# Attention on one Trainium2 core: the product of the probabilities with the values of a key block as one piece of up to 512 columns

## The chip, the core and the metric

The kernel runs on one NeuronCore of a Trainium2 chip. The core has TensorE (PE in the rows, with its weight loads as PEld), VectorE (DVE), ScalarE (ACT), GpSimdE (POOL) and SyncE (SP), which issues most DMAs. The metric is the device time of one execution in microseconds (us); lower is better. The times given are medians of several executions.

## The reference

The program is a small transformer stack on x of shape (1, 2048, 256): attention "a" (rotary, 16 query heads on 4 key heads), a feed-forward block with 4-bit weights, attention "b" (16 heads on 16), and the same feed-forward block again, each behind a layer norm and added to x. The change is in the attention, which both layers share:

```python
scores = jnp.einsum('bthd,bshd->bhts', q, k) * scale
causal = jnp.tril(jnp.ones((S, S), dtype=bool))
scores = jnp.where(causal[None, None, :, :], scores, -jnp.inf)
probs = jax.nn.softmax(scores, axis=-1)
attended = jnp.einsum('bhts,bshd->bthd', probs, v).reshape(B, S, hidden)
```

S is 2048, a head has 16 numbers, and all arithmetic is float32.

## The kernel before

**Tiles.** The 16 heads are worked in 4 groups g of 4 heads, the 2048 queries in 4 tiles t of 512. Groups follow each other with the tiles in the order 0, 1, 2, 3, then 3, 2, 1, 0, and so on. Keys are cut into blocks kb of 128; tile t needs blocks 0 to 4t+3, since attention is causal. In the last four of them queries below the block see none of its keys, so the block has only 512, 384, 256 or 128 columns there.

**Two passes over the scores.** The softmax needs each query's maximum before the exponential. So the scores are computed twice.

- M (line 856): queries by keys, for the maximum. One M is one head, 128 queries against a chunk of up to 512 keys. Two heads together make a pair: both halves of one slot of `ring`, and one VectorE reduction of 128x1024 (line 1071) reads them. `ring` has two slots, taken in turn, so the first half of a pair waits until the pair two before it has been reduced (`slot`, `pe.wait_ge(s_rd, n - 1)`). Chunks on the diagonal are 128 to 512 wide and get two small mask matmuls (line 860).
- S (line 882): keys by queries, 128 keys of one head against up to 512 queries, with the maximum folded in. ScalarE turns it into `probs` (line 976). S takes one of three banks `ps_s`; it waits for the exponential of the S three before it.
- PV (line 899): values times probabilities, one matmul per head, 4 heads side by side on 32 output rows each, added up over the key blocks in `ps_o`. A PV matmul is in float32, which the program turns into two records, so a piece of four heads shows as x8 in the trace.
- O (line 908): four transposes of the finished tile, through a slot of `ring`; VectorE divides (lines 1083 and 1086).

**The order of the work.** `attention_plan` writes one list of all this; each engine walks through it in order and issues its own part. A step is one key block: four S, one per head. While tile t is in its S pass, the M of the next tile are laid between its S, and the function `ahead` sets how many. From tile 3 of group 0 to the end of group 2, which is 96 steps in each layer, there is one M behind every S: the first half of a pair stands behind the S of heads 1 and 3, the second half behind the S of heads 2 and 0. In group 3 there are fewer and in its last two tiles none.

PV for a key block stands two steps behind its S. It is cut in two pieces of 256 columns: piece 0 ahead of the S of head 0, piece 1 ahead of the S of head 2. In the last two blocks of a tile only piece 1 is there, of 256 and of 128 columns; the block before them has a piece 0 of 128 columns.

Of the kernel before, what the change touches and what calls it, by code (L numbers as in the profile page):

```python
# [30 lines left out]
TW = 512  # L31
NT = S // TW
BT = TW // P
# [290 lines left out]
def attention_plan(extra):  # L324

    order = [(g, t) for g in range(NG) for t in (range(NT) if g % 2 == 0 else range(NT - 1, -1, -1))]
    pairs = [("M", g, t, qb, p, c) for g, t in order for qb in range(BT) for p in range(2) for c in range(t + 1)]
    first, ends, total = [], [], 0
    for g, t in order:
        first.append(total)  # L330
        total += BT * GH * (t + 1)
        ends.append(total)

    def ahead(s):
        tail = len(order) - NT
        if s < first[1]:
            return min(ends[1], LEAD + (ends[1] - LEAD) * s // (first[1] - 6))
        for k in range(1, len(order) - 1):
            if first[k] <= s < first[k + 1] and (k < NT - 1 or k >= tail):
                start, end = ends[k] + (SLACK if k > 1 else 0), ends[k + 1] + SLACK  # L340
                return min(total, start + (end - start) * (s - first[k]) // (first[k + 1] - first[k]))
        return min(total, max(e + SLACK - max(f - s, 0) for e, f in zip(ends, first)))

    plan, made, rows, turns = [], 0, [], []

    def after(x):
        if x[3:6] == (BT - 1, 1, x[2]):
            rows.append([("R", x[1], x[2]), 2 if x[1:3] == (0, 0) else 4])

    def pass_rows():  # L350
        for r in list(rows):
            r[1] -= 1
            if r[1] < 0:
                plan.append(r[0])
                rows.remove(r)

    def both_halves():
        x = pairs[made // 2]
        plan.extend([x + (0,), x + (1,)])
        after(x)  # L360
        pass_rows()
        return made + 2

    def pass_turns():
        for o in turns:
            o[1] -= 1

    def opening(t, counts, beside=(), after_turn=()):
        nonlocal made
        laid = relayout(t - 1, extra) if t else []  # L370
        items = projection(t, extra)
        for k, y in enumerate(items):
            plan.extend(laid[k] if k < len(laid) else [])
            plan.append(y)
            if k == 0:
                plan.extend(beside)
            if k == len(items) - 3:
                plan.extend([("TU", t + 1), *after_turn])
            for _ in range(counts[k - len(items)] if counts else 0):
                made = both_halves()  # L380

    plan += [("LS", 0), ("LC", 0, 1), ("N", 0), ("LS", 1)] + ([("W", 0)] if extra else [("F", 40)])
    plan += [("TU", 0), ("F", 12), ("LC", 1, 2), ("N", 1)]
    opening(0, [], [("LS", 2)], [("LS", 3), ("LC", 2, 4), ("N", 2)])
    opening(1, [0, 0, 2, 2], [], [("N", 3)])
    opening(2, [2, 2, 2, 2] if extra else [2, 3, 3])
    later = {}
    laid, items = relayout(NT - 2, extra), projection(NT - 1, extra)
    for k, y in enumerate(items):
        later[k * BT * GH // len(items)] = (laid[k] if k < len(laid) else []) + [y]  # L390
    for k, x in enumerate(relayout(NT - 1, extra)):
        later[BT * GH + 2 + 4 * k] = x
    turned = {30: ("WL", 1), 36: ("W", 1), 42: ("WL", 2), 50: ("W", 2), 56: ("WL", 3), 64: ("W", 3)} if extra else {}
    late, due, s, step = [], [], 0, 0
    for g, t in order:
        for kb in range(BT * (t + 1)):
            chunk, place = divmod(step - 13, 9)
            if extra and 0 <= chunk < NF and place == 0:
                plan.append(("X", chunk))
            k = step % (BT * NT * (NT + 1) // 2) - (3 if g else 8)  # L400
            if g + 1 < NG and 0 <= k < LOADS:
                plan.append(("LD", g + 1, k))
            if step in turned:
                due.append(turned[step])
            done = late.pop(0) if len(late) == LATE else None
            for h in range(GH):
                if done and h % 2 == 0:
                    at = done[2] - BT * done[1]
                    if at < 2 or h == (0 if at == BT - 1 else 2):
                        plan.append(("PV",) + done + (1 if at >= 2 else h // 2,))  # L410
                    if h:
                        pass_turns()
                    if h == 0 and at == BT - 1:
                        turns.append([("O",) + done[:2], 3])
                while rows and rows[0][0][1:] == (g, t):
                    pass_rows()
                due += later.get(s, [])
                if made % 2 == 0:
                    plan += due + [o for o, n in turns if n < 0]
                    due, turns = [], [o for o in turns if o[1] >= 0]  # L420
                plan.append(("S", g, t, kb, h))
                if made < ahead(s) or made % 2:
                    x = pairs[made // 2]
                    plan.append(x + (1 - h % 2,))
                    made += 1
                    if made % 2 == 0:
                        after(x)
                s += 1
                pass_rows()
                while made % 2 == 0 and made + 1 < ahead(s) - 1:  # L430
                    if g == 0:
                        plan.append(("FM", 2))
                    made = both_halves()
            if extra and chunk >= 0 and place == 8:
                plan.extend([("T", chunk, 0), ("T", chunk, 1)])
            late.append((g, t, kb))
            step += 1
    for done in late:
        for half in range(2):
            if half or done[2] - BT * done[1] < 2:  # L440
                plan.append(("PV",) + done + (half,))
    return order, plan + [o for o, _ in turns] + [("O",) + order[-1]]


# [82 lines left out]
def attention_block(nc, io, per, layer):  # L527
    rope = layer == "a"
    extra = rope
    with ExitStack() as ctx:  # L530
# [59 lines left out]
        order, plan = attention_plan(extra)  # L590
# [21 lines left out]
        half = [slice(HALF * h, HALF * (h + 1)) for h in range(2)]  # L612
# [32 lines left out]
        def width(t, kb):  # L645

            return P * max(0, kb - BT * t)
# [108 lines left out]
        def _(pe):  # L756
# [25 lines left out]
            for y in plan:  # L782
# [17 lines left out]
                elif y[0] == "TU":  # L800
                    t = y[1]
# [6 lines left out]
                elif y[0] == "PJ":  # L808
                    _, t, f = y
# [3 lines left out]
                    for a in range(2):  # L813
                        at, count = feats(f) if rope else ((2 * f + a) * P, P)
# [6 lines left out]
                elif y[0] == "VJ":  # L821
                    t = y[1]
                    out = slot(y)
                    at = 2 * P + 64 if rope else 4 * P
# [5 lines left out]
                elif y[0] == "RL":  # L830
                    _, t, f, a = y
                    n = part_no(("PJ", t, f))
                    b = n % NST
                    if n == 0:
# [7 lines left out]
                              start=False, stop=True).then_inc(s_s, 1)  # L842
                elif y[0] == "M":
                    _, g, t, qb, p, c, h = y
# [13 lines left out]
                    if c == t:  # L858
                        for a in range(2):
                            op = pe.matmul(out[:, h, w - P:w], ident[half[h], a, :], above[half[h], a, :],  # L860
                                           start=False, stop=a == 1)
                    if y in ends:
                        op.then_inc(s_rf, 1)
                elif y[0] == "R":
                    _, g, t = y
# [7 lines left out]
                elif y[0] == "S":  # L873
                    _, g, t, kb, h = y
                    out = bank(y)
                    if kb == 0 and h == 0:
# [7 lines left out]
                                   start=True, stop=not diagonal)  # L884
                    if diagonal:
                        for a in range(2):
                            op = pe.matmul(out[:, 0:P], ident[half[h % 2], a, :], below[half[h % 2], a, :],  # L887
                                           start=False, stop=a == 1)
                    op.then_inc(s_s, 1)
                elif y[0] == "PV":  # L890
                    _, g, t, kb, part = y
                    pe.wait_ge(s_e, scored[("S", g, t, kb, GH - 1)] + 1)
                    if kb == 0:
                        pe.wait_ge(s_ot, rank[g, t])
                    c = slice(max(width(t, kb), TW // 2 * part), TW // 2 * (part + 1))
                    n = pvs[y[:4]]
                    for h in range(GH):
                        v = vg[g][:, kb, 0:VC] if shared else vg[g][:, kb, h * VC:(h + 1) * VC]
                        last = pe.matmul(ps_o[32 * h:32 * h + VC, c], v, pr[n % NPR][:, h, c],  # L899
                                         start=kb == 0 and part == 0, stop=kb == BT * (t + 1) - 1)  # L900
                    if part:
                        last.then_inc(s_pv, 1)
                elif y[0] == "O":
                    _, g, t = y
                    pe.wait_ge(s_ot, rank[g, t] + 1)
                    out = slot(y)
                    for b in range(BT):
                        last = pe.transpose(out[:, 0, b * P:(b + 1) * P], ot[:, b * P:(b + 1) * P], per["ident"][:, :])
                    last.then_inc(s_rf, 1)
# [567 lines left out]
```

## Time and profile before

| | |
|---|---|
| median of 3 executions | 1894.46 us (1891.48 to 1908.91) |
| time of the profiled execution | 1903.19 us |
| its span, first to last instruction | 1901.3 us |
| mean granted TensorE clock | 0.946 |
| busy: PE, PEld | 1761.2 us (93%), 1135.2 us (60%) |
| busy: DVE, ACT, POOL | 1156.9 us (61%), 957.5 us (50%), 545.9 us (29%) |
| PE matmul records | 13822 |
| PV (line 899), records | 4608 |

"Span" is the time between the first and the last instruction of the profiled execution; the execution's own time is 1.9 us more. Busy is the time in which at least one instruction of the engine is under way. Matmuls are pipelined, so a busy PE is not a PE at its peak: the time that an instruction costs is better read from the distance between starts.

### The profile page before, as it was taken

How to read it: one execution, taken by the hardware profiler on the slowest of the kernel's cores; microseconds unless marked ns; L12 is line 12 of the kernel's file. 1: busy time of each engine (PE TensorE's matmuls, PEld its weight loads, DVE VectorE, ACT ScalarE, POOL GpSimd, SP SyncE). 2: the span in 40 equal slices, each digit the busy share in tenths (PEclk: the TensorE clock that was granted, in tenths of full speed). 3: DMA queues.
4: the chain of work that ended last, by engine and by line, in shares of the span. 5: the costliest groups of instructions: out<-in, count | busy, mean ns of one | idle time of the engine just before them, and what ended most of it. 6: DMA issues, size and time to landing. Idle time of an engine off the chain costs nothing. (4 is left out here: it accounts for less than half of the span.)

```text
span 1901.3 us, 34086 instructions
## 1 busy us (share of the span) xinstructions
PE 1761.2 (93%) x13822; PEld 1135.2 (60%) x13822; DVE 1156.9 (61%) x1702; ACT 957.5 (50%) x1901; POOL 545.9 (29%) x466
## 2 busy tenths in 40 slices
PE   7799999999999879999987999999999997999998
PEld 5554444554445568888865644445544446888887
DVE  5446777677875266444465477776777626654444
ACT  2133566666777524434332245776667872444333
POOL 5211566576677602223220010000000000223222
PEclk8786889999999889999998889999999998999999
DMA  5103305125011060000003223060330004100000
GB/s 130 50 27 42 54 22 104 40 55 87 23 42 39 34 266 1 1 1 0 0 1 117 84 37 54 10 82 2 44 48 2 2 2 201 66 12 1 11 11 11
DMA packets 49391, 86.04 MB, mean 45 GB/s; under 512 B 20856, under 2 KB 34936, under 8 KB 46984
## 3 DMA queue, kind: packets, MB, share of 16 engines
q1 hardware_dynamic: 44472, 67.84, 15.5%
q0 software_dynamic: 4256, 15.78, 2.7%
q8 instruction: 97, 1.59, 0.4%
q10 hardware_dynamic: 528, 0.52, 0.1%
q14 instruction: 38, 0.31, 0.1%
HBM read 55.02 MB, written 28.84 MB: 44 GB/s over the span
## 5 line engine op out<-in xcount | busy, mean ns | idle before, releaser
L1071 DVE TENSOR_REDUCE chunk_max<-ring 128x2 f32<-128x1024 f32 (+3 forms) x640 | 674.0, 1064 | 276.0 <-PE ring L856 162.8
L976 ACT ACTIVATE probs<-ps_s 128x512 f32<-128x512 f32 (+3 forms) x1280 | 624.1, 534 | 343.2 <-PE ps_s L887 177.5
L1404 POOL TENSOR_TENSOR inter_lo<-inter,inter_hi 128x512 fp32r<-128x512 f32 x128 | 165.4, 1292 | 935.4 <-ACT inter_hi L1338 935.4
L856 PE MATMUL ring<-unit_rounded 63*128 63x512 f32 (+3 forms) x640 | 246.1, 479 | 26.6 <-DVE chunk_max L1071 8.9
L856 PE MATMUL ring<-region_rounded 63*128 63x512 f32 (+3 forms) x640 | 254.9, 447 | 5.1 <-DVE chunk_max L1071 4.5
L882 PE MATMUL ps_s<-unit_rounded 64*128 64x512 f32 (+3 forms) x640 | 252.7, 446 | 5.4 <-ACT probs L976 4.2
L882 PE MATMUL ps_s<-region_rounded 64*128 64x512 f32 (+3 forms) x640 | 228.9, 441 | 4.3 <-ACT probs L976 4.2
L1378 DVE SCALAR_TENSOR_TENSOR gelu_a<-gelu_a,ps_g 128x512 f32<-128x512 f32 x128 | 87.9, 687 | 183.9 <-ACT gelu_a L1332 183.6
L882 PEld LDWEIGHTS ps_s<-unit_rounded 64*128 64x128 f32 x640 | 112.5, 195 | 138.8 <-ACT probs L976 105.9
L1332 ACT ACTIVATE gelu_a<-ps_g 128x512 f32<-128x512 f32 x128 | 76.5, 598 | 229.4 <-PE ps_u L94 229.2
L899 PE MATMUL ps_o<-probs,unit_plain 128*32 128x256 f32 (+1 forms) x2304 | 186.9, 398 | 0.0
L899 PE MATMUL ps_o<-probs,region_plain 128*32 128x256 f32 (+1 forms) x2304 | 177.3, 380 | 0.0
L882 PEld LDWEIGHTS ps_s<-region_rounded 64*128 64x128 f32 x640 | 101.8, 184 | 126.5 <-ACT probs L976 102.9
L92 PE MATMUL ps_d<-w_mlp,inter_lo 128*128 128x256 f32 x512 | 150.2, 293 | 28.8 <-DVE x L1369 15.2
L94 PE MATMUL ps_d<-w_mlp,inter_hi 128*128 128x256 f32 x512 | 145.3, 284 | 0.0
L93 PE MATMUL ps_d<-w_mlp,inter_hi 128*128 128x256 f32 x512 | 144.9, 283 | 0.0
L856 PEld LDWEIGHTS ring<-unit_rounded 63*128 63x128 f32 x640 | 104.8, 195 | 64.0 <-DVE chunk_max L1071 21.9
L1345 ACT ACTIVATE gelu_b<-gelu_a 128x512 f32<-128x512 f32 x128 | 80.9, 632 | 118.5 <-DVE gelu_a L1378 118.5
L1383 DVE SCALAR_TENSOR_TENSOR gelu_b<-gelu_b,ps_g 128x512 f32<-128x512 f32 x128 | 87.9, 687 | 85.3 <-ACT gelu_b L1345 85.3
L860 PE MATMUL ring<-mask_above,half_ident 64*128 64x128 bf16 x1024 | 138.3, 228 | 0.0
L887 PE MATMUL ps_s<-mask_below,half_ident 64*128 64x128 bf16 x1024 | 133.3, 225 | 0.0
L92 PEld LDWEIGHTS ps_d<-w_mlp,inter_lo 128*128 128x128 f32 x512 | 97.6, 191 | 52.7 <-POOL inter_lo L1404 31.4
(184 smaller groups left out, 2980.3 us busy)
## 6 DMA issues: line engine op xcount, KB each, us to landing
w_mlp<-w_scr SPq DMA_DIRECT2D x32, 768.0 KB, 14.6
w_scr<-region_rounded POOLq DMA_DIRECT2D x16, 768.0 KB, 3.9
region_rounded<-q_scr SPq DMA_DIRECT2D x24, 256.0 KB, 8.3
q_scr<-region_rounded SPq DMA_DIRECT2D x16, 192.0 KB, 2.3
unit_rounded<-q_scr SPq DMA_DIRECT2D x12, 256.0 KB, 8.9
q_scr<-region_rounded SPq DMA_DIRECT2D x8, 384.0 KB, 3.6
k_scr<-region_rounded SPq DMA_DIRECT2D x8, 384.0 KB, 3.6
v_scr_b<-region_plain SPq DMA_DIRECT2D x4, 768.0 KB, 3.7
```

What stands on the lines that cost most here:

```text
L92: pe.matmul(out, ll, rh, start=start, stop=False)
L93: pe.matmul(out, lh, rl, start=False, stop=False)
L94: return pe.matmul(out, lh, rh, start=False, stop=stop)
L856: op = pe.matmul(out[:, h, 0:w], qt[g][plain[h], p, q0:q0 + P], kt[g][plain[h], p % NKP, c * TW:c * TW + w], start=True, stop=c < t)
L860: op = pe.matmul(out[:, h, w - P:w], ident[half[h], a, :], above[half[h], a, :], start=False, stop=a == 1)
L882: op = pe.matmul(out[:, 0:TW - w0], kt[g][shifted[h % 2], (h // 2) % NKP, kb * P:(kb + 1) * P], qt[g][shifted[h % 2], h // 2, t * TW + w0: ...
L887: op = pe.matmul(out[:, 0:P], ident[half[h % 2], a, :], below[half[h % 2], a, :], start=False, stop=a == 1)
L899: last = pe.matmul(ps_o[32 * h:32 * h + VC, c], v, pr[n % NPR][:, h, c], start=kb == 0 and part == 0, stop=kb == BT * (t + 1) - 1)
L976: act.activation(pr[n % NPR][:, h, w0:TW], src[:, 0:TW - w0], ACT.Exp, scale=SCALE).then_inc(s_e, 1)
L1071: dve.tensor_reduce(mp[rank[y[1:3]] % 2][:, qb, 2 * p:2 * p + 2, c], ring[n % 2][:, :, 0:w], AX.X, ALU.max).then_inc(s_rd, 1)
L1378: dve.scalar_tensor_tensor(out=ta[b][:, :], in0=ta[b][:, :], scalar=1.0, in1=ps_g[b][:, :], op0=ALU.add, op1=ALU.mult).then_inc(s_arg, 1)
L1404: pool.tensor_tensor(il[n % NI][:, :], ti[n % 2][:, :], ih[n % NI][:, :].bitcast(F32), ALU.subtract).then_inc(s_il, 1)
```

## The change

The two pieces of a key block's PV become one, ahead of the S of head 0, with 512 columns, or 384, 256 or 128 in the last four blocks of a tile. So the PV of the third block on the diagonal, which was one piece ahead of the S of head 2, moves ahead of the S of head 0 as well. Everything else stands in the list where it stood. Each layer has 160 pieces where it had 288.

```diff
             for h in range(GH):
-                if done and h % 2 == 0:
+                if done and h == 0:
                     at = done[2] - BT * done[1]
-                    if at < 2 or h == (0 if at == BT - 1 else 2):
-                        plan.append(("PV",) + done + (1 if at >= 2 else h // 2,))
-                    if h:
-                        pass_turns()
-                    if h == 0 and at == BT - 1:
+                    plan.append(("PV",) + done + (1,))
+                    if at == BT - 1:
                         turns.append([("O",) + done[:2], 3])
+                if done and h == 2:
+                    pass_turns()
...
     for done in late:
-        for half in range(2):
-            if half or done[2] - BT * done[1] < 2:
-                plan.append(("PV",) + done + (half,))
+        plan.append(("PV",) + done + (1,))
...
-                    c = slice(max(width(t, kb), TW // 2 * part), TW // 2 * (part + 1))
+                    c = slice(width(t, kb), TW)
                     n = pvs[y[:4]]
                     for h in range(GH):
...
-                                         start=kb == 0 and part == 0, stop=kb == BT * (t + 1) - 1)
+                                         start=kb == 0, stop=kb == BT * (t + 1) - 1)
```

TensorE's instructions in the stage with one M per S, layer b, group 2, tile 2, from the S of head 1 of one step to that of head 0 two steps on. `ps_s0` to `ps_s2` are the three banks of S, `ring0` and `ring1` the two slots of the pairs, `ps_o` is PV. Before:

```order
L882 MATMUL ps_s2_8<-unit_rounded_8 128x512
L856 MATMUL ring1_8<-unit_rounded_8 128x512
L899 MATMUL ps_o_8<-probs_8,unit_plain_8 32x256 x4
L882 MATMUL ps_s0_8<-unit_rounded_8 128x512
L856 MATMUL ring1_8<-unit_rounded_8 128x512
L882 MATMUL ps_s1_8<-unit_rounded_8 128x512
L856 MATMUL ring0_8<-unit_rounded_8 128x512
L899 MATMUL ps_o_8<-probs_8,unit_plain_8 32x256 x4
L882 MATMUL ps_s2_8<-unit_rounded_8 128x512
L856 MATMUL ring0_8<-unit_rounded_8 128x512
```

The change at the same place:

```order
L879 MATMUL ps_s2_8<-unit_rounded_8 128x512
L853 MATMUL ring1_8<-unit_rounded_8 128x512
L879 MATMUL ps_s0_8<-unit_rounded_8 128x512
L853 MATMUL ring1_8<-unit_rounded_8 128x512
L879 MATMUL ps_s1_8<-unit_rounded_8 128x512
L853 MATMUL ring0_8<-unit_rounded_8 128x512
L896 MATMUL ps_o_8<-probs_8,unit_plain_8 32x512 x4
L879 MATMUL ps_s2_8<-unit_rounded_8 128x512
L853 MATMUL ring0_8<-unit_rounded_8 128x512
```

Before, each of the two slots has a piece of PV between the first and the second half of its pair. In the change the pair in `ring1` has none between its halves, and the pair in `ring0` has the whole piece of 512 columns.

The second place is on TensorE too: layer b, group 3, tile 1, where no M are left. Before:

```order
L899 MATMUL ps_o_8<-probs_8,region_plain_8 32x256 x4
L882 MATMUL ps_s2_8<-region_rounded_8 128x512
L882 MATMUL ps_s0_8<-region_rounded_8 128x512
L899 MATMUL ps_o_8<-probs_8,region_plain_8 32x256 x4
L882 MATMUL ps_s1_8<-region_rounded_8 128x512
L882 MATMUL ps_s2_8<-region_rounded_8 128x512
L899 MATMUL ps_o_8<-probs_8,region_plain_8 32x256 x4
```

The change at the same place:

```order
L896 MATMUL ps_o_8<-probs_8,region_plain_8 32x512 x4
L879 MATMUL ps_s2_8<-region_rounded_8 128x512
L879 MATMUL ps_s0_8<-region_rounded_8 128x512
L879 MATMUL ps_s1_8<-region_rounded_8 128x512
L879 MATMUL ps_s2_8<-region_rounded_8 128x512
L896 MATMUL ps_o_8<-probs_8,region_plain_8 32x512 x4
```

All four S of a step now follow one another, and the fourth is written to the bank of the first (`ps_s2`).

## Rows read from the trace of the kernel before

**Rows 1.** The page: its head and the busy time of each engine.

```profile
span 1901.3 us, 34086 instructions
PE 1761.2 (93%) x13822; PEld 1135.2 (60%) x13822; DVE 1156.9 (61%) x1702; ACT 957.5 (50%) x1901; POOL 545.9 (29%) x466
```

**Rows 2.** Windows: stretch, length, busy time of each engine, granted clock.

```profile
core 0: us, PE busy (x) PEld busy (x) DVE busy (x) ACT busy (x) POOL busy (x), PEclk, DMA share, GB/s
...
237.70:541.00 303.30, 294.45 (x2900) 152.16 (x2897) 229.19 (x264) 206.54 (x425) 202.59 (x146) 0.97 0.26 55
...
1059.40:1182.60 123.20, 113.62 (x902) 57.79 (x901) 82.64 (x83) 53.85 (x108) 7.57 (x3) 0.90 0.31 54
1182.60:1466.50 283.90, 276.23 (x2821) 141.05 (x2817) 213.38 (x221) 195.68 (x403) 0.00 (x0) 1.00 0.23 31
1466.50:1539.30 72.80, 71.84 (x775) 34.96 (x773) 42.84 (x47) 57.67 (x117) 0.00 (x0) 1.00 0.01 2
```

**Rows 3.** Waits: who waited for whom; us in total, times, longest.

```profile
PEld ring L856 <- DVE chunk_max L1071: 40.2, 98, 2.0
...
PE ring L856 <- DVE chunk_max L1071: 13.4, 38, 1.7
```

**Rows 4.** Timeline of PE, layer b: start, us, engine, line, operation, names, shapes.

```profile
1403.03 0.50 PE L882 MATMUL ps_s<-unit_rounded 64*128 64x512 f32 x1
1403.03 0.73 PE L856 MATMUL ring<-unit_rounded 63*128 63x512 f32 x2
1403.37 0.40 PE L882 MATMUL ps_s<-unit_rounded 64*128 64x512 f32 x1
...
1404.84 0.48 PE L882 MATMUL ps_s<-unit_rounded 64*128 64x512 f32 x1
1404.88 0.49 PE L856 MATMUL ring<-unit_rounded 63*128 63x512 f32 x1
1405.30 0.64 PE L899 MATMUL ps_o<-probs,unit_plain 128*32 128x256 f32 x8
...
1405.87 0.49 PE L856 MATMUL ring<-unit_rounded 63*128 63x512 f32 x1
```

**Rows 5.** Timeline of DVE in the same stretch.

```profile
1403.60 1.23 DVE L1071 TENSOR_REDUCE chunk_max<-ring 128x2 f32<-128x1024 f32 x1 [0.39 <-PE ring L856]
```

**Rows 6.** Timeline of DVE, layer b, group 2, tile 3; x2 are two in a row.

```profile
1423.64 2.36 DVE L1071 TENSOR_REDUCE chunk_max<-ring 128x2 f32<-128x1024 f32 x2 [0.59 <-PE ring L856]
1426.48 1.95 DVE L1071 TENSOR_REDUCE chunk_max<-ring 128x2 f32<-128x1024 f32 x2 [0.48 <-PE ring L856]
1429.32 2.46 DVE L1071 TENSOR_REDUCE chunk_max<-ring 128x2 f32<-128x1024 f32 x2 [0.89 <-PE ring L856]
1432.17 1.96 DVE L1071 TENSOR_REDUCE chunk_max<-ring 128x2 f32<-128x1024 f32 x2 [0.40 <-PE ring L856]
...
1435.75 2.46 DVE L1071 TENSOR_REDUCE chunk_max<-ring 128x2 f32<-128x1024 f32 x2 [0.83 <-PE ring L856]
```

**Rows 7.** Timeline of PE: a piece of 128 columns and what follows it.

```profile
1382.12 0.43 PE L899 MATMUL ps_o<-probs,unit_plain 128*32 128x128 f32 x8
1382.47 0.32 PE L882 MATMUL ps_s<-unit_rounded 64*128 64x128 f32 x1
```

**Rows 8.** Timeline of PE in group 3, tile 1, where no M are left.

```profile
1548.56 0.64 PE L899 MATMUL ps_o<-probs,region_plain 128*32 128x256 f32 x8
1549.13 0.51 PE L882 MATMUL ps_s<-region_rounded 64*128 64x512 f32 x2
...
1549.70 0.64 PE L899 MATMUL ps_o<-probs,region_plain 128*32 128x256 f32 x8
```

**Rows 9.** Timeline of ACT in the stretch of rows 4.

```profile
1403.56 0.60 ACT L976 ACTIVATE probs<-ps_s 128x512 f32<-128x512 f32 x1 [0.53 <-PE ps_s L882]
```

**Rows 10.** Timeline of PE at a granted clock of 0.5 (1.2 GHz).

```profile
1107.68 1.08 PE L899 MATMUL ps_o<-probs,unit_plain 128*32 128x256 f32 x8
1108.69 0.79 PE L882 MATMUL ps_s<-unit_rounded 64*128 64x512 f32 x1
```

## The prediction, made before the changed kernel was run

> **What bounds the kernel now.** The page comes first [rows 1]: PE is busy 93% of the span and every other engine 61% or less. The list of waits seems to confirm that: PE's matmuls wait for VectorE's reduction in only 38 places, 13.4 us, and its weight loads 40.2 us [rows 3]. Read so, a change that takes work off PE gains. The windows show which stage counts [rows 2]: group 0 from its tile 3 to the end of group 2 takes 303.3 us in layer a and 283.9 us in layer b for 96 steps each, so 3.16 and 2.96 us a step, at clock 0.97 and 1.00. VectorE is busy 213 of the 283.9 us there, so it isn't the bound by its sum.
>
> The timeline says what is. Follow one slot of `ring` [rows 4, 5]. The second half of a pair starts at 1403.03; VectorE begins its reduction at 1403.60 and ends it at 1404.83; the first half of the next pair in that slot starts at 1404.88; PV starts at 1405.30, and the second half at 1405.87. That closes a loop: 0.57 + 1.23 + 0.05 + 0.42 + 0.57 = 2.84 us, and it allows one step per turn, since each slot serves one pair a step. PE shows as busy all this time, since its records overlap (the M of 1404.88 lasts 0.49 us, PV starts 0.42 behind it) and S runs beside a late M; so the wait hardly shows as idle PE. The reductions of tile 3 in group 2 begin at 1423.64, 1426.48, 1429.32, 1432.17 [rows 6]: 2.84, 2.84, 2.85 us, the loop to the hundredth, with VectorE idle for 0.4 to 0.9 us ahead of each. So the stage is bound by a latency round PE and VectorE, and PV's duration is a term of it.
>
> **What the change does to PE's own work.** A piece of 256 columns takes 1405.30 to 1405.87, 0.569 us before rounding; one of 128 takes 1382.12 to 1382.47, 0.356 us [rows 4, 7]. So 128 columns cost 0.213 us and a piece 0.143 us besides. One of 512 columns is then 0.569 + 2 x 0.213 = 0.995 us; 384 gives 0.782. No row shows a piece of 512. Its bounds are 0.569 + 0.213 = 0.78 us, if only half of the added columns cost, and 2 x 0.569 = 1.14, if nothing is saved; I take 0.995, since two widths fix the line. 256 pieces go (2 x 128), so PE alone would save 256 x 0.143 = 36.6 us.
>
> The Trainium skill (TensorEngine Tiling, "Key Properties") says that a change of tiling mode drains TensorE. By that page each piece between S and S pays such a drain, and the whole change would be worth its 256 drains. The trace agrees that there is a fixed part, 0.143 us a piece.
>
> **What it does to the loop.** The order shows it: the pair of one slot has no PV between its halves any more, the pair of the other has all 512 columns. Its loop is 0.57 + 1.23 + 0.05 + 0.42 + 0.995 = 3.27 us. The light slot's is 0.57 + 1.23 + 0.05 + 0.34 (S to S, 1403.03 to 1403.37) = 2.19 us, but a step ends only when both are done. PE does nothing in between: the waiting M stands ahead of PV in PE's queue, and behind PV all S. So a step goes from 2.84 to 3.27 us, +0.43, where the heavy slot's pair is a full one.
>
> I counted by the order over the 192 steps of this stage (two layers), with the step lengths from the starts of S in the trace:
> - 108 steps with a full pair in the heavy slot and 512 columns, without O. 74 last 2.83 to 2.98 us now; they become 3.27: 74 x 0.41 = +30. The other 34 last 3.09 to 5.9 us, because masks, layer a's unpacking on VectorE or a tile's change add to them; they get +0.43 at the most and -0.143 at the least. I take 0, since 3.27 is about what they take already.
> - 14 steps with O, which takes a slot of its own, so the first half waits for the pair just before: 1432.17 to 1435.75 is 3.58 us [rows 6]. The longer PV lies behind that wait too: 14 x 0.43 = +6.
> - 16 steps with a full pair and a PV of 256 columns, which moves from the S of head 2 to that of head 0, into the heavy loop: from 2.35 to 2.84 us, +0.49 each, +8.
> - 12 with a full pair and 384 columns (0.57 + 1.23 + 0.05 + 0.42 + 0.78 = 3.05, now 2.80): +3.
> - 42 others, with short pairs or a PV of 128 columns; 22 of them have 512 or 384 columns and save 0.143: -3.
>
> Stage: +44 us.
>
> **The rest.** Group 0's tiles 0 to 2 take 123.2 us in layer b for 24 steps [rows 2], with up to four pairs a step. If PE bounds them, 18 steps a layer save 0.143 us (-5 in all); if a slot's loop with PV in it does, 24 of the 48 lose up to 0.43 (+10). I take +3, between the two. In group 3 the three banks of S take over. Half a step without M lasts 1.14 us [rows 8], a step 2.28. After: the exponential starts 0.53 us behind its S (1403.03 to 1403.56) and lasts 0.60 [rows 9]; the fourth S needs its bank, so it starts at 0.53 + 0.60 + 0.05 = 1.18 us; PV follows 0.34 later, taken as from S to S, then 0.995: 2.51 us. That is +0.23 in 12 steps, +3. Where M are left, 28 steps a layer take 72.8 us in layer b [rows 2], 2.60 each; the 44 with 512 columns come to 2.51, -4. ScalarE pays nothing else: PV's own inputs are exponentials of two steps back. Both feed-forward phases and the projections don't change.
>
> Sum: 44 + 3 + 3 - 4 = +46 us on the profiled execution's 1903.2 us. That one is 8.7 us above the median, which is 1894.5; taken on the median it gives **1941 us**.
>
> **Rivals.**
> - *The gain arrives* (0.08). If the loop had slack, for instance because M could be issued under a running PV, the time is 1894.5 - 36.6 = 1858 us. For it: PE's 93%. Against it: starts 2.84 us apart with VectorE idle. It decides from the point where a 512-column loop fits under a step's own work on PE, which is 4 x 0.34 + 0.995 = 2.4 us. The Trainium skill (Perfetto Trace Analysis, "Matmuls") holds larger matmuls to be more efficient where they are possible; it speaks for this rival, and rows 6 speak against it.
> - *Gain and loss cancel* (0.12). The 74 steps pay, but PE-bound steps save the whole 0.143 wherever they can: 30 - (256 - 74) x 0.143 = +4, so 1899 us, and up to 1913.
> - *The clock falls too* (0.06). PE's idle share grows in each step. At 1.2 GHz a piece of 256 takes 1107.68 to 1108.69, 1.01 us, not 0.57 [rows 10]; one of 512 about 1.86. The loop is then 0.87 longer, and with slower S and M 1.1. A third of the 192 steps at it is 70 us more: about 2012 us. Against it: the stage runs at clock 1.00 now, though some of its steps take 4 us and more.
> - *The forecast* (0.74): the long PV sits in one slot's loop. Its own range: with only the 74 steps paying and a saving in all other 82 merged pieces of the stage, 30 - 12 = +18, so 1912; with all 122 full steps at +0.43 (52), +11 for the moved and shortened pieces, +10 early and +3 late, +76, so 1971.
>
> **How the numbers follow.** The range 1908 to 1972 holds the forecast's range and the upper part of the cancelling case; it leaves out the gain, the clock and the rest of that case, 0.2. About 1%, 19 us, is what a measurement of this kernel can tell from no change. Slower by more: the forecast and the clock, 0.80; within: the cancelling case, 0.12; faster: 0.08.
>
> **What would show it.** In the new profile: PV in 2560 records, a piece of 512 columns 0.995 us from its start to the next S; reductions of 1024 columns in group 2, tile 3 that come in twos, 3.27 us apart, with more than 0.8 us idle ahead; that tile, now 46.3 us, at 51 or more; PE waiting more for line 1071 than the 53.6 us of rows 3; in group 3, tile 1, steps near 2.5 us and ScalarE no longer the engine without gaps. I am wrong if steps there come in under 2.84 us, or if PV of 512 columns costs under 0.6 us.

## The result and the profile after

| | before | the change |
|---|---|---|
| median | 1892.97 us (1891.39 to 1908.91, 4 executions) | 1951.14 us (1948.78 to 1955.25, 4 executions) |
| ratio to before | | 1.0278, 95% interval 1.0226 to 1.0330 |
| profiled execution, its span | 1903.19 us, 1901.3 us | 1948.78 us, 1946.9 us |
| mean granted clock | 0.946 | 0.955 |

The kernel is 2.8% slower. Line numbers are lower by 3: M is line 853, S 879, PV 896, the exponential 973, the pairs' reduction 1068. The page of the change, its head, its busy row, and the groups of the reduction and of the two sorts of M. A group shows busy time and mean ns, and then the idle time ahead of it with its releasers:

```profile
span 1946.9 us, 29958 instructions
...
PE 1741.7 (89%) x11774; PEld 1100.6 (57%) x11774; DVE 1135.6 (58%) x1702; ACT 937.0 (48%) x1901; POOL 545.8 (28%) x466
...
L1068 DVE TENSOR_REDUCE chunk_max<-ring 128x2 f32<-128x1024 f32 (+3 forms) x640 | 656.8, 1061 | 335.8 <-PE ring L853 237.3
...
L853 PE MATMUL ring<-unit_rounded 63*128 63x512 f32 (+3 forms) x640 | 219.9, 455 | 39.8 <-DVE chunk_max L1068 20.4
L853 PE MATMUL ring<-region_rounded 63*128 63x512 f32 (+3 forms) x640 | 237.1, 428 | 20.3 <-DVE chunk_max L1068 17.6
```

PE has 2048 matmul records less than in [rows 1] and is busy 19.5 us less; it did save work. Yet the span grew by 45.6 us, and every engine's share fell. The list of waits says who waits for whom:

```profile
PEld ps_s L879 <- ACT probs L973: 270.5, 442, 1.7
DVE chunk_max L1068 <- PE ring L853: 237.3, 229, 7.4
...
PEld ring L853 <- DVE chunk_max L1068: 86.9, 175, 0.8
...
PE ring L853 <- DVE chunk_max L1068: 38.0, 143, 0.6
```

PE now waits 86.9 + 38.0 = 124.9 us for the reductions, where [rows 3] had 53.6, and VectorE waits 237.3 us for M, where it was 162.8. Each waits for the other: a loop.

Windows of the change, with the columns of rows 2: layer a from group 0, tile 3 to the end of group 2; layer b's group 0, tiles 0 to 2; the same stage in layer b; and the two tiles of group 3 with M.

```profile
226.00:552.10 326.10, 292.10 (x2278) 143.04 (x2274) 219.83 (x264) 200.35 (x425) 205.55 (x147) 0.99 0.24 52
1070.80:1194.20 123.40, 109.47 (x764) 53.83 (x763) 82.38 (x83) 53.29 (x109) 7.58 (x3) 0.92 0.32 54
1194.20:1504.60 310.40, 277.89 (x2198) 133.36 (x2194) 205.91 (x221) 188.97 (x402) 0.00 (x0) 1.00 0.21 28
1453.40:1504.60 51.20, 45.84 (x338) 20.40 (x334) 34.78 (x36) 32.04 (x66) 0.00 (x0) 1.00 0.00 1
1504.60:1578.40 73.80, 70.37 (x582) 32.08 (x578) 42.26 (x46) 55.32 (x116) 0.00 (x0) 1.00 0.01 1
```

Against [rows 2] the stage takes 326.1 instead of 303.3 us in layer a and 310.4 instead of 283.9 in layer b: +22.8 and +26.5, together more than the 45.6 us by which the span grew. Layer b's early tiles are as long as they were (123.4 and 123.2 us). The fourth row is group 2, tile 3 alone, 51.2 us. VectorE, in that tile:

```profile
1456.60 2.36 DVE L1068 TENSOR_REDUCE chunk_max<-ring 128x2 f32<-128x1024 f32 x2 [1.07 <-PE ring L853]
1459.87 1.82 DVE L1068 TENSOR_REDUCE chunk_max<-ring 128x2 f32<-128x1024 f32 x2 [0.92 <-PE ring L853]
1463.14 2.36 DVE L1068 TENSOR_REDUCE chunk_max<-ring 128x2 f32<-128x1024 f32 x2 [1.44 <-PE ring L853]
1466.40 1.82 DVE L1068 TENSOR_REDUCE chunk_max<-ring 128x2 f32<-128x1024 f32 x2 [0.91 <-PE ring L853]
```

The twos start 3.27, 3.27 and 3.26 us apart, with 0.91 to 1.44 us idle ahead; they were 2.84 apart [rows 6]. One such step on PE:

```profile
1461.15 0.49 PE L853 MATMUL ring<-region_rounded 63*128 63x512 f32 x1 [0.17 <-DVE chunk_max L1068]
1461.57 1.07 PE L896 MATMUL ps_o<-probs,unit_plain 128*32 128x512 f32 x8
1462.57 0.49 PE L879 MATMUL ps_s<-unit_rounded 64*128 64x512 f32 x1
1462.57 0.73 PE L853 MATMUL ring<-region_rounded 63*128 63x512 f32 x2
1462.91 0.62 PE L879 MATMUL ps_s<-unit_rounded 64*128 64x512 f32 x2
...
1463.75 0.50 PE L879 MATMUL ps_s<-unit_rounded 64*128 64x512 f32 x1 [0.21 <-ACT probs L973]
1464.42 0.49 PE L853 MATMUL ring<-region_rounded 63*128 63x512 f32 x1 [0.17 <-DVE chunk_max L1068]
```

The waiting first half comes at 1461.15 and again at 1464.42, 3.27 us later. PV takes 1461.57 to the second half at 1462.57, 1.00 us. The reduction starts at 1463.14, 0.57 us behind it, and the next first half follows its end. There is a second wait in the same step: the fourth S (1463.75) waits for the exponential that frees its bank. Counted over the program, the S that start within 75 ns of that end were 66 before and are 239 now. This wait comes first and is covered by the reduction's: the same wait stands in e1 below, where a step takes 2.61 us and not 3.27.

To compare the stages I added up all steps by the starts of S, both layers, in each profile ("early" is group 0, tiles 0 to 2; "main" the stage of 192 steps with an M behind every S; "group 3" runs to the start of its last step). The experiments are in the same table:

| kernel | early | main | group 3 | median us |
|---|---|---|---|---|
| before | 260.3 | 587.2 | 201.8 | 1892.97 |
| the change | 247.4 | 636.4 | 210.1 | 1951.14 |
| e1, one piece ahead of S of head 1 | 235.6 | 534.4 | 208.9 | 1833.7 |
| e2, two pieces ahead of S of heads 1, 3 | 220.7 | 526.6 | 205.7 | 1803.26 |
| e3, two pieces ahead of S of head 0 | 259.6 | 647.0 | 209.4 | 1951.35 |
| e5, a longer reduction | 314.7 | 732.0 | 209.6 | 2106.39 |
| e6, one piece in group 3 only | 258.8 | 587.0 | 210.7 | 1906.6 |
| e8, one piece ahead of S of head 2 | 249.0 | 611.8 | 209.1 | 1922.89 |
| e9, e2 with the block of 384 as one piece | 222.3 | 528.5 | 203.9 | 1808.15 |

### The profile page after: what moved, and what is told of

Its sections match the earlier page's. It is cut to its first block and busy times, and to the rows that moved or that the text cites. A ratio compares the mean times of both kernels' runs of the same rounds, so it can differ in the third digit from the quotient of the medians.

```text
span 1946.9 us, 29958 instructions
## 1 busy us (share of the span) xinstructions
PE 1741.7 (89%) x11774; PEld 1100.6 (57%) x11774; DVE 1135.6 (58%) x1702; ACT 937.0 (48%) x1901; POOL 545.8 (28%) x466
## 5 line engine op out<-in xcount | busy, mean ns | idle before, releaser
L1068 DVE TENSOR_REDUCE chunk_max<-ring 128x2 f32<-128x1024 f32 (+3 forms) x640 | 656.8, 1061 | 335.8 <-PE ring L853 237.3
L973 ACT ACTIVATE probs<-ps_s 128x512 f32<-128x512 f32 (+3 forms) x1280 | 602.2, 538 | 402.2 <-PE ps_s L879 214.2
L853 PE MATMUL ring<-unit_rounded 63*128 63x512 f32 (+3 forms) x640 | 219.9, 455 | 39.8 <-DVE chunk_max L1068 20.4
L853 PE MATMUL ring<-region_rounded 63*128 63x512 f32 (+3 forms) x640 | 237.1, 428 | 20.3 <-DVE chunk_max L1068 17.6
L879 PE MATMUL ps_s<-unit_rounded 64*128 64x512 f32 (+3 forms) x640 | 234.9, 424 | 12.6 <-ACT probs L973 10.1
L896 PE MATMUL ps_o<-probs,unit_plain 128*32 128x512 f32 (+3 forms) x1280 | 155.5, 559 | 0.0
L896 PE MATMUL ps_o<-probs,region_plain 128*32 128x512 f32 (+3 forms) x1280 | 152.6, 551 | 0.0
L853 PEld LDWEIGHTS ring<-unit_rounded 63*128 63x128 f32 x640 | 99.6, 189 | 85.0 <-DVE chunk_max L1068 44.9
L853 PEld LDWEIGHTS ring<-region_rounded 63*128 63x128 f32 x640 | 109.0, 185 | 50.6 <-DVE chunk_max L1068 42.0
L857 PE MATMUL ring<-mask_above,half_ident 64*128 64x128 bf16 x1024 | 131.2, 226 | 0.0
```

Of the source, the lines that this page charges most:

```text
L853: op = pe.matmul(out[:, h, 0:w], qt[g][plain[h], p, q0:q0 + P], kt[g][plain[h], p % NKP, c * TW:c * TW + w], start=True, stop=c < t)
L879: op = pe.matmul(out[:, 0:TW - w0], kt[g][shifted[h % 2], (h // 2) % NKP, kb * P:(kb + 1) * P], qt[g][shifted[h % 2], h // 2, t * TW + w0: ...
L973: act.activation(pr[n % NPR][:, h, w0:TW], src[:, 0:TW - w0], ACT.Exp, scale=SCALE).then_inc(s_e, 1)
L1068: dve.tensor_reduce(mp[rank[y[1:3]] % 2][:, qb, 2 * p:2 * p + 2, c], ring[n % 2][:, :, 0:w], AX.X, ALU.max).then_inc(s_rd, 1)
```

## The experiments

The theory: PV's duration is a term of the loop second half, reduction, first half, PV, second half in one slot. What counts is where the long piece stands, not that it is one piece. The rivals: joining costs something by itself (the drain, PE's queue), or the loss is in another wait (the banks of S).

**e1: the one piece elsewhere.** Behind S of head 0 comes a second half, behind S of head 1 a first one. So a piece ahead of the S of head 1 lies between two pairs, and between the halves of none.

```diff
-                if done and h == 0:
+                if done and h == 1:
```

> The change with the one piece moved by one place: it stands ahead of the S of head 1, where no pair of M is open, and all else stays. Theory (PV's length is a term of the loop of the slot whose pair it stands in): no pair has PV between its halves, so from a second half to the next first half of that slot there are 2.0 us of other work, more than the 1.84 us of the wait. A full step is then set by PE, the three banks of S or VectorE's two reductions, about 2.5 us, not 3.27: the stage with one M per S falls from 636 us to about 530, the time from 1951 to about 1845 us. Rival (the longer matmuls or the run of four S cost by themselves, wherever they stand): 1951 us, within 10.

Measured: 1833.7 us (1828.1 to 1839.1), ratio 0.9676 [0.9594, 0.9759] to before, whose median beside it was 1901.6. The piece is the same as in the change, and four S still follow one another; the place is the only difference. It is worth 117 us by the medians, 114 by the ratios (before's median was 1893.0 us beside the change). One step in e1, group 2, tile 3, on PE (lines as in the change):

```profile
1359.62 0.50 PE L879 MATMUL ps_s<-unit_rounded 64*128 64x512 f32 x1
...
1360.81 0.50 PE L879 MATMUL ps_s<-unit_rounded 64*128 64x512 f32 x1 [0.22 <-ACT probs L973]
...
1361.25 1.06 PE L896 MATMUL ps_o<-probs,unit_plain 128*32 128x512 f32 x8
1362.24 0.50 PE L879 MATMUL ps_s<-unit_rounded 64*128 64x512 f32 x1
```

No M waits in this step; what is left is the bank. The S of 1360.81 waits for its bank, 1.19 us behind the first of the four; PV follows 0.44 later and lasts 0.99: 2.62 us. The median of the full steps is 2.61.

**e2: the two pieces elsewhere.** The kernel before, with its pieces ahead of the S of heads 1 and 3, so each lies between two pairs, and S is spread evenly too.

```diff
-                if done and h % 2 == 0:
+                if done:
                     at = done[2] - BT * done[1]
-                    if at < 2 or h == (0 if at == BT - 1 else 2):
+                    if h % 2 and (at < 2 or h == (1 if at == BT - 1 else 3)):
                         plan.append(("PV",) + done + (1 if at >= 2 else h // 2,))
-                    if h:
+                    if h == 2:
                         pass_turns()
```

> The kernel before with its two pieces moved by one place each, ahead of the S of heads 1 and 3, so that no pair has PV between its halves; nothing is joined. Theory: the loop of 2.84 us is gone, a full step takes about 2.5 us (PE's own 2.47), the time falls from 1893 to about 1845 us. Rival (before was bound by PE's own work, not by the loop): 1893 us, within 5.

Measured: 1803.26 us (1802.2 to 1807.9), ratio 0.9515 [0.9438, 0.9592]. It is the fastest of all, 4.9% below before. The expectation was 1845 us and missed by 42: it counted the full steps of the main stage, but the table gives 60.6 us there and 39.6 in the early tiles. Part of those 39.6 is the clock. Not all is: in e6, whose code is that of before in these tiles, layer b's early tiles take 115.0 us at a clock of 1.00, and in e2 105.6 at 0.97. So PV's place counts there too. On PE, group 2, tile 3 (lines as before):

```profile
1339.99 0.50 PE L882 MATMUL ps_s<-unit_rounded 64*128 64x512 f32 x1
1339.99 0.73 PE L856 MATMUL ring<-region_rounded 63*128 63x512 f32 x2
1340.33 0.40 PE L882 MATMUL ps_s<-unit_rounded 64*128 64x512 f32 x1
1340.66 0.64 PE L899 MATMUL ps_o<-probs,unit_plain 128*32 128x256 f32 x8
1341.23 0.50 PE L882 MATMUL ps_s<-unit_rounded 64*128 64x512 f32 x1
```

Half a step is 1.24 us, a step 2.48, and no row has a wait: 4 x 0.335 for the S with their M and 2 x 0.569 for PV are 2.48. In such a step PE's own work is the bound. Such steps are only a part of the stage: the 108 steps that are full ones in the change have a median of 2.60 us in e2, 2.61 in e1, since the masks of a diagonal chunk and waits add to others; what bounds those was not taken apart. PE's window over that tile, with the columns of rows 2:

```profile
1322.50:1364.10 41.60, 41.53 (x449) 19.35 (x445) 36.26 (x36) 33.09 (x66) 0.00 (x0) 1.00 0.01 2
```

PE is busy 41.53 of 41.60 us, but it was busy 45.15 of 46.30 in the same tile of before, so this alone would not tell. Over the whole span its share is 93%, just what it is in [rows 1] at a span 101 us longer.

**e3: two pieces, both where the change has its one.** This takes joining and place apart.

```diff
-                if done and h % 2 == 0:
+                if done and h == 0:
...
-                    if at < 2 or h == (0 if at == BT - 1 else 2):
-                        plan.append(("PV",) + done + (1 if at >= 2 else h // 2,))
+                    plan.extend([("PV",) + done + (half,) for half in range(0 if at < 2 else 1, 2)])
```

> The move without the joining: both pieces of 256 columns stand ahead of the S of head 0, one behind the other. Theory: the loop holds 2 x 0.569 us of PV if a piece pays its fixed 0.143 us behind another piece too: full steps 3.41 us, 0.14 more than the change, the time about 1975 us. If the fixed part is paid only at a change between S and PV (a drain at the mode's change), full steps 3.27 us and 1951 us. Rival (the joining is what costs, not the place): near 1893 us.

Measured: 1951.35 us (1946.8 to 1966.1), ratio 1.0280 [1.0196, 1.0363]. That is the time of the change. (In the table e3's main stage is 10.6 us longer than the change's; in its profile the clock was 0.85 in group 2, tile 3, where the change had 1.00, and that tile took 56.4 us, not 51.2; other tiles of its layer b stage had a lower clock too.) Both pieces on PE in e3:

```profile
1456.13 1.07 PE L899 MATMUL ps_o<-probs,unit_plain 128*32 128x256 f32 x16
1457.13 0.44 PE L882 MATMUL ps_s<-unit_rounded 64*128 64x384 f32 x1
```

Two pieces back to back take 1.00 us, as one of 512 does, not 2 x 0.569 = 1.14. The fixed 0.143 us is paid once for each visit to PV, not for each piece. So joining brings nothing that can be measured by itself, and the effect of the change is the place. The Trainium skill (TensorEngine Tiling, "Key Properties") puts the drain on a change of tiling mode; these rows agree, 0.143 us at each such visit and next to none between two pieces of one mode. They show where this price falls, not what it is made of.

**e5: the reduction made longer.** The change, with a second VectorE reduction ahead of each of the pairs', over the first quarter of the columns.

```diff
+                at = 64 * (rank[y[1:3]] % 2) + 2 * (8 * qb + 4 * p + c)
+                dve.tensor_reduce(extra_max[:, at:at + 2], ring[n % 2][:, :, 0:w // 4], AX.X, ALU.max)
```

> The change with VectorE's part of the loop made longer: ahead of each reduction of a pair stands a second one over the first quarter of its columns, whose result nobody reads (0.43 us where the pair is full). PE's and ScalarE's work is the same, and VectorE would have room: 2 x (1.23 + 0.43) = 3.3 us. Theory (the loop holds the reduction): a full step goes from 3.27 to about 3.68 us, the stage with one M per S from 636 to about 710 us, the time to about 2040 us with the first tiles' share. Rival (VectorE is beside the path, as its 58% busy time says): 1951 us, within 5.

Measured: 2106.39 us (2095.8 to 2110.8), ratio 1.1058 [1.0962, 1.1153]. VectorE in group 2, tile 3 of e5 (the extra one is line 1070), and then PE there:

```profile
1619.99 0.43 DVE L1070 TENSOR_REDUCE extra_max<-ring 128x2 f32<-128x256 f32 x1 [1.25 <-PE ring L854]
1620.33 1.22 DVE L1071 TENSOR_REDUCE chunk_max<-ring 128x2 f32<-128x1024 f32 x1
...
1623.59 0.42 DVE L1070 TENSOR_REDUCE extra_max<-ring 128x2 f32<-128x256 f32 x1 [0.58 <-PE ring L854]
```

```profile
1621.60 0.49 PE L854 MATMUL ring<-region_rounded 63*128 63x512 f32 x1 [0.49 <-DVE chunk_max L1071]
1622.02 1.07 PE L897 MATMUL ps_o<-probs,unit_plain 128*32 128x512 f32 x8
1623.02 0.50 PE L880 MATMUL ps_s<-unit_rounded 64*128 64x512 f32 x1
```

The extra reduction costs 0.34 us, and the step grows from 3.27 to 3.60 us (1619.99 to 1623.59), although VectorE still idles 1.25 and 0.58 us ahead of its twos. So the reduction's length is a term of the loop too, one for one; the median of the 108 full steps went from 3.28 to 3.62. The time missed the expected 2040 us by 66, though. The main stage is 95.6 us longer than the change's, with a clock of 0.92 and 0.94 in the two layers where the change had 0.99 and 1.00, and the early tiles are 67.3 us longer, at a clock of 0.71 and 0.74 (0.96 and 0.92 in the change). How much of that is the clock and how much the loop is not shown.

**e6: one piece in group 3 alone**, where hardly any M are left and only the banks can bind.

```diff
+                    if done[0] == NG - 1:
+                        if h == 0:
+                            plan.append(("PV",) + done + (2,))
...
+                    c = slice(width(t, kb), TW) if part == 2 else slice(max(width(t, kb), TW // 2 * part), TW // 2 * (part + 1))
```

> The kernel before, with PV in one piece ahead of the S of head 0 in group 3 alone, where few M or none are left; groups 0 to 2 as before. Read by stage, not by its time. Theory (the fourth S of a row waits for the exponential of the first, three banks): steps without M go from about 2.25 to 2.6 us, group 3 from 202 us (both layers) to about 208, the stage with one M per S stays at 587. Rival (PE bounds group 3): 44 joined pieces save 0.143 us each, about 195 us.

Measured, one execution: 1906.6 us against 1907.2 for before beside it. The main stage is unchanged (587.0), group 3 takes 210.7 us instead of 201.8; 2.5 of that is layer b's last tile, at a clock of 0.70. PE in group 3, tile 1 of e6:

```profile
1540.90 1.06 PE L900 MATMUL ps_o<-probs,region_plain 128*32 128x512 f32 x8
1541.90 0.73 PE L883 MATMUL ps_s<-region_rounded 64*128 64x512 f32 x3
1543.08 0.49 PE L883 MATMUL ps_s<-region_rounded 64*128 64x512 f32 x1 [0.45 <-ACT probs L977]
1543.50 1.06 PE L900 MATMUL ps_o<-probs,region_plain 128*32 128x512 f32 x8
```

The fourth S comes 1.18 us behind the first, as the prediction had it. PV follows 0.42 later, and a step is 2.60 us. So in group 3 the banks lose the saving and more; but it is a small part of the whole.

**e8: the one piece ahead of the S of head 2**, which is the mirror of the change: now the other slot's pair has it between its halves.

```diff
+                if done and h == 2:
+                    plan.append(("PV",) + done + (1,))
                 if done and h == 0:
                     at = done[2] - BT * done[1]
-                    plan.append(("PV",) + done + (1,))
```

> The change with the one piece two places on, ahead of the S of head 2, inside the pair of the other slot. Theory: that slot's loop is now 3.27 us, so full steps and the time are those of the change, 1951 us, within 8, although the piece stands only one place behind that of the kernel with it ahead of head 1 (1834 us). Rival (what counts is how early PV stands, or the order against the exponentials): about 1830 us, or between.

Measured, one execution: 1922.89 us, 28 below what the theory expected by symmetry. This one missed. VectorE in group 2, tile 3 of e8 (M is line 854 there, its masks 858):

```profile
1449.05 2.09 DVE L1069 TENSOR_REDUCE chunk_max<-ring 128x2 f32<-128x768 f32 x2 [1.03 <-PE ring L858]
1452.05 2.36 DVE L1069 TENSOR_REDUCE chunk_max<-ring 128x2 f32<-128x1024 f32 x2 [0.91 <-PE ring L854]
1455.43 2.09 DVE L1069 TENSOR_REDUCE chunk_max<-ring 128x2 f32<-128x768 f32 x2 [1.02 <-PE ring L858]
```

The twos begin 3.00 and 3.38 us apart, in turn. The two slots are not alike. While M for a tile 3 are laid, pairs of chunk 0 and 2 fall on the one slot and those of chunk 1 and 3 on the other, and chunk 3 is the one on the diagonal, 128 to 512 columns wide. The change holds PV in the slot whose pairs are full there; e8 holds it in the one where they are often narrow. I sorted the 138 steps of the main stage that begin with a PV of 512 columns (from that PV to the next) by the width of the pair that has this PV between its halves:

| | full pair | narrower pair |
|---|---|---|
| the change | 120 steps, 418.5 us, mean 3.49 | 18 steps, 53.9 us, mean 2.99 |
| e8 | 76 steps, 260.4 us, mean 3.43 | 62 steps, 193.9 us, mean 3.13 |

The price of a full one is about the same in both, and e8 has 44 fewer of them. The 138 steps together take 472.4 and 454.3 us, which is 18.1 of the 24.6 us between the two main stages; the rest lies in the steps with a narrower PV. So the loop can stand, and the symmetry that I had assumed doesn't. This is an explanation after the fact, from one profile, and no run tests it.

**e9: e2 with the block of 384 columns as one piece** of PV ahead of the S of head 1, which spares one visit to PV in 18 steps of the main stage.

```diff
+                    if h == 1 and at == 1:
+                        plan.append(("PV",) + done + (2,))
```

> The kernel with the halves ahead of heads 1 and 3 (1803 us), with one thing joined: in the key block of 384 columns the pieces of 128 and 256 are one ahead of the S of head 1. Theory (that kernel's steps are set by PE's own work, and short S leave the banks free): 0.143 us saved in each of 32 steps, 1799 us. Rival (the banks or VectorE bind there): 1803 us, no change; the two can hardly be told apart by the time, but by the steps' length, 2.82 to 2.68 us with a full pair.

Measured: 1808.15 us (1801.4 to 1812.5), ratio 0.9494 [0.9414, 0.9575], main stage 528.5 against e2's 526.6. The expected 4 us are less than these executions scatter. The 18 steps with the joined piece take 40.6 us in e9's profile and 44.7 in e2's, so 0.23 less each; the other 174 steps take 487.8 and 481.9. So the saving comes in its own steps, but the stage as a whole doesn't keep it. Why not is open.

## Why the prediction came out right, point by point

- **The bound (right).** That the stage is a loop through one slot with PV as a term was read from starts 2.84 us apart with VectorE idle, against a page that says 93%. The change, e1, e3 and e5 show it from four sides: PV longer, +0.43 us a step; PV out of the loop, 2.61; PV as long but in two pieces, the same; the reduction 0.34 longer, +0.33. e8, expected at the change's time, is the one that did not fit as it was put.
- **The piece of 512 (right).** 0.995 us was predicted from two widths. 1461.57 to 1462.57 in the rows above, and 0.996 between the unrounded starts; 384 columns take 0.782, as predicted.
- **Full steps with 512 columns.** +30 was predicted over 108 steps, +34.8 measured (332.2 to 367.0 us); their median went from 2.85 to 3.28. The split was miscounted: 81 of them last 2.83 to 2.98 us in the trace of before, not 74, and 27 last longer. The 81 rose by 34.8, 0.43 each; the 27 together stayed at 100.2 us, as I had put them.
- **Steps with O.** +6 predicted for 14, +2.8 measured. They rose by 0.20 us in the mean, not 0.43, and from -0.05 to 0.43 one by one: so part of the longer piece is covered there.
- **The moved piece of 256 columns (two errors).** 18 such steps by the count in the traces rose from 42.2 to 52.8, +10.6, where I had +8 for 16. But a step that a piece enters is one that another loses: the steps that end with the PV of 128 columns had the piece of 256 inside, and fell from 64.2 to 55.1, -9.1. I had listed those under "others", with nothing.
- **Short pairs (wrong sign).** They were to save 0.143 each. The 16 steps with 512 columns and a narrow pair rose from 44.6 to 50.1, +5.5. A pair 256 columns wide (8 of the 16) has a reduction of 0.69 us, and its loop with the long PV is 0.57 + 0.69 + 0.05 + 0.42 + 0.995 = 2.73 us, above the 2.53 that these steps took; their median is now 2.83. With the steps of 128 columns (-9.1) and 6 narrow ones of 384 (-0.6) these others come to -4.1, against -3 predicted, but only since two errors cancel.
- **The stage.** +44 predicted, +49.2 measured (with +5.1 for the 12 full steps with 384 columns, +3 predicted).
- **Early tiles (the sign differs, by the clock).** +3 predicted, -12.9 measured: -13.1 in layer a, +0.2 in layer b. In layer b's tile 2, where both have a clock of 0.96, the change costs 2.2 us (46.0 to 48.2). In layer a the clock hides what the loop did, as the windows of before over layer a's tiles 1 and 2 and of the change over its tile 1 show (PEclk is the third number from the end):

```profile
135.00:185.30 50.30, 47.99 (x316) 21.82 (x315) 31.32 (x32) 18.84 (x37) 8.81 (x8) 0.73 0.20 27
185.30:237.70 52.40, 47.77 (x383) 23.12 (x384) 39.80 (x44) 26.33 (x51) 25.22 (x20) 0.85 0.40 62
```

```profile
136.30:176.90 40.60, 36.12 (x266) 16.66 (x266) 30.49 (x32) 18.40 (x37) 8.81 (x8) 1.00 0.25 33
```

  Tile 1 had a clock of 0.73 before and 1.00 after, and it took 9.7 us less. A clock that differs from one execution to the next is also the likely reason, not a shown one, why the spans differ by 45.6 us and the medians by 58.2: the profiled execution of before took 10.2 us more than the median that stands in the table above, that of the change 2.4 us less.
- **Group 3 (too low).** -1 predicted, +8.3 measured. The 12 steps with 512 columns and no M rose from 30.5 to 35.6 us, +5.1 where I had +3: such a step is 2.61 us, not 2.51, since PV follows a waiting S after 0.42 us and not 0.34, and several took 2.18 before, not 2.28. The 44 with M rose from 120.9 to 124.9, where I had -4: I had taken 2.60 for each of them before, but many took 2.47 to 2.6, and 2.61 is now the least nearly everywhere. 2.6 of the 8.3 are again the clock: by the steps of the table layer b's last tile takes 9.8 us where before took 7.2. With its last step it is 14.8 at a clock of 0.63, against 11.1 at 1.00 (e1, which has the long piece too, takes 11.2 at 1.00).

The windows of the change over group 3's last two tiles in layer b:

```profile
1578.40:1598.80 20.40, 18.40 (x149) 8.00 (x145) 3.27 (x5) 15.05 (x34) 0.00 (x0) 1.00 0.00 1
1598.80:1613.60 14.80, 13.52 (x96) 6.55 (x92) 0.63 (x2) 7.12 (x18) 0.00 (x0) 0.63 0.01 2
```

- **The sum (near, in part by luck).** +46 predicted, +45.6 in the spans. Stage and group 3 together were 14.5 us too low, and the early tiles 15.9 too high, which is mostly the clock. The medians differ by 58.2, and 1951 lies 10 us above the forecast.
- **The signs to look for.** PV has 2560 records; twos 3.27 us apart with 0.91 us or more idle; tile 3 of group 2 at 51.2 us; 124.9 us of waiting where 53.6 was. All came. ScalarE has gaps in group 3: it is busy 15.05 of the 20.40 us of tile 1.
- **The rivals.** The gain did not arrive, since there was no slack in that slot; e1, with the piece elsewhere, is 3.2% faster than before; but e2, with nothing joined, is faster still, so that is the place and not the rival's gain. Gain and loss did not cancel. The clock was as high in the main stage as before (0.99 and 1.00).

Where I stopped short: the prediction named the loop and costed the change in it, and didn't ask where PV would be in no loop at all. The same rows answer that.

## What to carry to other kernels

Where two engines hand a few buffers back and forth, look at which instructions of the in-order queue stand between the refilling of a buffer and the instruction that completes it: they are part of the latency loop, however independent their data are. Long independent work belongs between two buffers' fills, not between the halves of one; here that place alone was worth about 115 us with one piece (e1 against the change) and 5% with two (e2 against before). A busy share of 93% was the same with this loop in the stage and without it; equal distances between starts, longer than the engine's own work in a step (2.84 against 2.48 us here) and with the partner idle ahead of them, tell the two apart.

## What the runs showed of the hardware

- The fixed 0.143 us of a PV piece is paid once for a run of pieces of the same 128x32 shape, with S and M (64 rows) around it, and not for each piece: 0.569 us for one of 256 columns, 1.00 us for two in a row (e3). Cutting this work into pieces cost 0.005 us a step as long as they stood together.
- The granted clock of the early tiles differs from one profile to the next. In e5 tile 1 of layer a ran at 0.63 and took 57.7 us, where the change took 40.6 at 1.00:

```profile
140.70:198.40 57.70, 53.92 (x267) 22.30 (x266) 39.50 (x61) 18.92 (x37) 8.83 (x8) 0.63 0.18 26
```

- The same tile of before ran at 0.73 in one profile and in e6, whose code is the same there, at 0.58. Before's executions scatter from 1882 to 1911 us, more than group 3 or the early tiles are worth; medians of a few executions and the sums by stage had to be read together. What decides the clock in these tiles stays open.
- An S that waits for its bank starts 53 ns after the end of the exponential, an M that waits for its slot 53 to 56 ns after the end of the reduction: the commonest values, much the same in all these kernels.
- Shortening the reduction (e4, the change with a reduction over half the columns, expected at 1870 us) gave no time, so the loop's term is shown by lengthening alone.
